# A graph network on one core: small weight loads issued behind the prologue's rounds, the bias add on VectorE tile by tile, and scatters behind the last gather without a wait for sums

## The chip, the cores and the metric

The kernel runs on one core of a Trainium2 chip. It is one program with five instruction streams: TensorE (PE, matrix products), VectorE (DVE), ScalarE (ACT), GpSimd (POOL) and SyncE (SP, which only issues transfers). Each stream runs in the order in which it is written, and the streams meet at semaphores. The metric is the device time of one execution in microseconds (us); lower is better.

## The reference

Four graph layers follow each other on 3750 nodes with 256 features and 63750 edges sorted by destination. Each layer normalises the nodes, clips at zero, computes something over the edges and adds it to `x`:

```
h = relu(layernorm(x));  x = x + L0(h, src, dst, edge_type)    # attention over 8 relations, 4 heads, + h_bias
h = relu(layernorm(x));  x = x + L1(h, ...)                    # graph convolution to 10 clusters, softmax
h = relu(layernorm(x));  x = x + L2(h, edge_attr, ...)         # edge net, sum over neighbours, 3-layer net
h = relu(layernorm(x));  x = x + L3(h, ...)                    # mean over neighbours, two products

feat_all = einsum('ni,rhid->rnhd', h, conv_weights)            # L0
e     = leaky_relu(el[type, src] + er[type, dst]);  alpha = softmax of e over the edges of one dst
out   = segment_sum(alpha * feat_all[type, src], dst) + h_bias
```

The change touches the beginning (L0's table and the dense adjacency matrix) and the scatters that fill this matrix.

## The kernel before, in words

Nodes stand in NT = 30 tiles of 128, edges in T = 500 tiles of 128. The work that matters here comes in this order.

**Load and normalise.** SP loads the edges, `x` and the attention weights. GpSimd writes zeros over the adjacency matrix `a_d` in DRAM (30 stores of 1088 KB, line 556; semaphore `a_zero`). ScalarE normalises the 30 node tiles (line 632), TensorE turns each (`turn_ring`, line 896; semaphore `n0_tp`) and computes the attention columns (line 928), VectorE copies the turned tiles (line 1453) and between them works on one-row masks (`follow_rows`, line 1403). GpSimd adds `h_bias` to all of `X` at once (line 561, 128x7680) as soon as ScalarE has read `X`, and stores the sum as `xb_d` (line 592; semaphore `x_out`).

**The prologue's rounds.** 50 rounds of 10 edge tiles. For a round SP loads two broadcast rows of `rel_d` (`rel_rows`) and one of `key_d` (`key_rows`); all SP loads have line 360. From the first VectorE makes one half of a one-hot matrix (`dst_one_hot`, line 1514) and ScalarE the other (lines 652 and 653). TensorE multiplies it (lines 965 and 966), and in the same stream computes the 120 parts of the feature table (line 954), which ScalarE copies out (line 667) and stores as `feat_d` (line 674). VectorE reduces (line 1533), counts equal edges (line 1520) and writes the values `VAL` (line 1527; semaphore `val_ready`). The loads for a round are issued when the one-hots two rounds before have been made. GpSimd scatters the values into `a_d`, four tiles a round, 200 in all (line 575); the first waits for `a_zero`, each fourth for `val_ready`. SP's twelve loads of small weights (`small_in`: W1A, EW2, CE, GB, COL, COL8) are issued ahead of the first `key_rows`, and VectorE waits for all twelve ahead of the first round. The four loads into COL8 have elements of 4 bytes, 1024 to a load.

**The gathers.** When all of `feat_d` is written and the 200 scatters are issued, GpSimd gathers the source rows of the 500 edge tiles (line 586) into a ring of 60 and, from tile 85 on, issues two scatters among five gathers. The other engines do softmax, messages and sums behind it, 20 tiles to a batch (DVE line 1671 adds the sums of a tile). Behind the last gather stand the 133 scatters left, each of which waits until one more tile has been summed (`agg_ps`).

**Behind that** the sums are turned home into `X`, the layer of clusters multiplies the adjacency matrix, which SP loads from `a_d` (line 360 into BG), and the edge network and the last layer follow.

The lines are those of the profile before.

Of the kernel before, what the change touches and what calls it, by code (L numbers as in the profile page):

```python
# [13 lines left out]
P = 128  # L14
# [3 lines left out]
ALU = mybir.AluOpType  # L18
ACT = mybir.ActivationFunctionType
# [27 lines left out]
def gnn(nc, x, src, dst, edge_attr, edge_type, conv_w, attn_l, attn_r, h_bias, gcn_w, gcn_b, cluster,  # L47
        eps, ee_w1, ee_b1, ee_w2, ee_b2, w1, b1, g1, be1, w2, b2, g2, be2, w3, b3, bn_g, bn_b,
        gamma, beta, w_l, b_l, w_r, out):
    N, D = x.shape  # L50
# [7 lines left out]
    NT = -(-N // P)  # L58
# [12 lines left out]
    NB = 20  # L71
# [17 lines left out]
    with ExitStack() as ctx:  # L89
# [184 lines left out]
        def s(name):  # L274
            if name not in S:
                S[name] = sem(name)
            return S[name]
# [71 lines left out]
        def bc(ap, shape):  # L349
            return ap.broadcast_to(shape)  # L350
# [7 lines left out]
        def _(sp):  # L358
# [53 lines left out]
                    rel_rows(u, u, h)  # L412
            for h in range(H):
                softmax_rows(h)
            with nc.allow_non_contiguous_dma(reason="small weight columns"):
                load(W1A[0:ED, :], ee_w1, "small_in")
                load(W1A[ED:ED + 1, :], ee_b1.rearrange("(o n) -> o n", o=1), "small_in")
                load(EW2[:, :, :], ee_w2.rearrange("(c p) n -> p c n", p=P), "small_in")
                load(CE[:, :], cluster, "small_in")
                load(GB[:, :], row(gcn_b, P), "small_in")  # L420
                load(B2C, ee_b2.rearrange("(c p) -> p c", p=P), "small_in")
                load(B1C, ee_b1.rearrange("(c p) -> p c", p=P), "small_in")
                load(SC2, eps.partition_broadcast(P), "small_in")
                for i, a in enumerate((g1, be1, g2, be2)):
                    load(COL8[:, i, :], a.rearrange("(c p) -> p c", p=P), "small_in")
# [5 lines left out]
            with sp.Fori(1, IT // 2) as w:  # L431
                for b in range(2):
# [5 lines left out]
                    sp.wait_ge(s("val_ready"), u + 1)  # L438
                    key_rows(u, b)

            sp.wait_ge(s("x_out"), 16)
            for v in range(NE):
                if v >= 3:
# [97 lines left out]
        def _(pool):  # L541
# [14 lines left out]
                pool.dma_start(rows(a_d, t).rearrange("p (a n) -> p a n", a=2),  # L556
                               bc(ZRO.unsqueeze(1), [P, 2, AD // 2])).then_inc(s("a_zero"), 16)

            pool.wait_ge(s("hb_in"), 16)
            pool.wait_ge(s("n0_hr"), NT)  # L560
            pool.tensor_tensor(X[:, :, :], X[:, :, :], bc(HB.unsqueeze(1), [P, NT, D]), ALU.add).then_inc(s("x_biased"), 1)
            pool.wait_ge(s("n0_tp"), NT)
            step(pool.memset(SEL, 0.0))
            for a in range(3):
# [8 lines left out]
            def scatter(t):  # L573

                pool.indirect_dma_start(  # L575
                    a_d.rearrange("n (w o) -> (n w) o", o=1), bass.IndirectOffsetOnAxis(ap=IDXS[:, t:t + 1], axis=0),
                    VAL[:, t:t + 1], None,
                ).then_inc(a_set[chunk_of(t)], 16)
                if t in CHUNKS[1:4]:
                    pool.wait_ge(a_set[chunk_of(t)], 16)  # L580
# [7 lines left out]
                    bass.IndirectOffsetOnAxis(ap=IDXST[:, t:t + 1], axis=0),  # L588
                ).then_inc(rows_in[t // NB % 3], 16)

            pool.wait_ge(s("x_biased"), 1)
            pool.dma_start(xb_d.rearrange("(t p) d -> p t d", p=P), X[:, :, :]).then_inc(s("x_out"), 16)
            pool.wait_ge(s("a_zero"), 16 * NT)
            for t in range(SOON):
                if t % CT == 0:
                    pool.wait_ge(s("val_ready"), t // CT + 3)
                scatter(t)
            pool.wait_ge(s("dve_mark"), DVE_MARKS["er_all"])
            pool.wait_ge(s("idx_ready"), 2)
# [9 lines left out]
            for t in range(T):  # L609
                gather(t)  # L610
                if t >= LEAD and (t - LEAD + 1) * 2 // 5 > (t - LEAD) * 2 // 5:
                    scatter_late(counted)
                    counted += 1
            for i, n in enumerate(range(counted, TR)):
                pool.wait_ge(s("agg_ps"), 20 + min(T - 3 * NB + 2 + i, T))
                scatter_late(n)
            pool.wait_ge(s("l3_d"), 7 * (NJ - 1) + 1)
            pool.memset(SG, 0.0).then_inc(s("acc_zero"), 1)  # L618
# [2 lines left out]
        def _(act):  # L621
# [52 lines left out]
                act.dma_start(rows(feat_d, t), STAGE[:, i, :, :].rearrange("p r n -> p (r n)")).then_inc(s(f"stage_out{i}"), 16)  # L674

            assert highs == 2 * IT
            act.wait_ge(s("small_in"), 16 * 12)
            act.activation(B1C, B1C, ACT.Relu).then_inc(s("b1_relu"), 1)
            for i in range(2):
                act.wait_ge(s(f"stage_out{i}"), 16 * NJ)  # L680
            act.wait_ge(s("cont_ready"), 1)
# [34 lines left out]
                edge_relu(0, q)  # L716
            soft_exp(0)
            soft_take(0)
            for b in range(NS):
                act.wait_ge(s("ex_sb"), b + 1)  # L720
                for k in range(NB):
                    v = (NB * b + k) // 4
                    if b + 1 < NS and k == 12:
                        soft_exp(b + 1)
                    for q in range(H):
                        m = RING[:, b % 3, k, q * DH:(q + 1) * DH]
                        last = act.activation(m, m, ACT.Copy, scale=EXT[:, b % 2, k, 1 + q:2 + q])  # L727
                    last.then_inc(s("msg_ready"), 1)
                    if k % 4 == 0 and v >= 1:
                        edge_relu(v, 1)  # L730
                    if k % 4 == 2 and v + 1 < NE:
                        edge_relu(v + 1, 0)
                    if k % 4 == 3 and v + 2 < NE:
                        edge_turned(v + 2)
                    if b + 1 < NS and k == 16:
                        soft_take(b + 1)
# [157 lines left out]
        def _(pe):  # L894
# [167 lines left out]
            pe.wait_ge(s("dve_mark"), DVE_MARKS["edge_start"])  # L1062
            net_turn(0)
            net_turn(1)
            for q in range(2):
                hidden(0, q)
            for part in (soft_turn, soft_ends, soft_carry, soft_back):
# [288 lines left out]
        def _(dve):  # L1356
# [189 lines left out]
                    counts(u + 1, following[0])  # L1546
                    values(u + 1)

            dve.wait_ge(s("small_in"), 16 * 12)
            for h in range(2):  # L1550
                dst_one_hot(0, h, 0, 0)
            counts(0, 0)
            values(0)
            for u in range(IT - 1):
                er_step(u, ((u + 1) % 2, (u + 1) // 2))
            er_step(IT - 1)

            dve.wait_ge(s("x_out"), 16)
# [175 lines left out]

            def home():

                step(ts(TILE0, IOTA[0:LT, 0:NT], -float(P), None, ALU.mult))
                attention_weights()
                dve.wait_ge(s("x_back0"), 16)
# [314 lines left out]
```

## Time and profile before

| | us |
|---|---|
| median of three runs | 3149.1 |
| lowest and highest | 3144.74 and 3156.03 |
| the profiled execution | 3144.03 |
| its span, first to last instruction | 3142.2 |

The granted TensorE clock was 0.937 of full speed on average. Busy shares of the span, from the page:

| engine | busy us | share |
|---|---|---|
| TensorE products | 2824.6 | 90% |
| VectorE | 1831.0 | 58% |
| ScalarE | 1405.3 | 45% |
| GpSimd | 1043.2 | 33% |

A busy share over the whole program says little here, since the stages have different limits: the page's 40 slices show 9 tenths for TensorE nearly everywhere, except in the first two slices (78.6 us each), which read 3 and 4. GpSimd reads 6 to 7 from the fourth slice to the seventeenth and almost nothing behind the nineteenth. The transfer engines read 8, 9, 7, 7 in the first four slices. The change works in the first six slices and between the seventeenth and the nineteenth. The small numbers in square brackets in a row are idle time of the engine just before the instruction, and the arrow names what ended it.

### The profile page before, as it was taken

How to read it: one execution, taken by the hardware profiler on the slowest of the kernel's cores; microseconds unless marked ns; L12 is line 12 of the kernel's file. 1: busy time of each engine (PE TensorE's matmuls, PEld its weight loads, DVE VectorE, ACT ScalarE, POOL GpSimd, SP SyncE). 2: the span in 40 equal slices, each digit the busy share in tenths (PEclk: the TensorE clock that was granted, in tenths of full speed). 3: DMA queues.
4: the chain of work that ended last, by engine and by line, in shares of the span. 5: the costliest groups of instructions: out<-in, count | busy, mean ns of one | idle time of the engine just before them, and what ended most of it. 6: DMA issues, size and time to landing. Idle time of an engine off the chain costs nothing.

```text
span 3142.2 us, 47689 instructions
## 1 busy us (share of the span) xinstructions
PE 2824.6 (90%) x14970; PEld 1862.6 (59%) x15034; DVE 1831.0 (58%) x5208; ACT 1405.3 (45%) x3883; POOL 1043.2 (33%) x1049
## 2 busy tenths in 40 slices
PE   3499958999999999988679998899999999999998
PEld 2344427899999888874144444555555555545446
DVE  7487866888888777775054333355555555513334
ACT  2077866778777888852032000244444444400000
POOL 4266677777777777777000000000000000000000
PEclk6599978999999999977869999999999999999999
DMA  8977754333333333216814333200000000132232
GB/s 295 343 219 204 223 158 117 96 94 95 93 94 92 93 93 94 68 54 181 253 63 123 101 103 98 75 5 7 3 7 5 5 7 3 49 101 68 84 101 79
DMA packets 245039, 317.67 MB, mean 101 GB/s; under 512 B 117627, under 2 KB 165924, under 8 KB 240740
## 3 DMA queue, kind: packets, MB, share of 16 engines
q1 hardware_dynamic: 191412, 179.07, 20.7%
q0 software_dynamic: 49104, 104.11, 11.1%
q10 hardware_dynamic: 4320, 31.95, 2.6%
q8 instruction: 108, 1.77, 0.2%
q14 instruction: 95, 0.78, 0.1%
HBM read 237.42 MB, written 77.59 MB: 100 GB/s over the span
## 4 chain that ended last, share of the span: by engine, by line
PE 63%; DVE 12%; ACT 7%; issue 5%; DMA 5%; SPq 4%; DVEq 3%; POOL 1%; POOLq 0%
PE PS L1237 17%; PE PS L1080 15%; PE PS L954 7%; PE PS L1046 5%; PE PS L1021 4%; PE PS L1059 4%; SPq L360 3%; PE PS L896 3%; DMA BG<-a_d 3%; ACT BG L727 3%; DVE BG L1805 2%; DVEq L1686 2%; DVE SUMS L1671 2%; ACT SL L810 1%; POOL BG L586 1%
## 5 line engine op out<-in xcount | busy, mean ns | idle before, releaser
L575 POOL DMA_INDIRECT a_d<-VAL,IDXS x499 | 501.1, 1004 | 236.9 <-issue 146.0
L1237 PE MATMUL PS<-BG,SL 128*128 128x512 f32 (+1 forms) x1440 | 538.4, 530 | 12.2 <-ACT SL L810 12.2
L586 POOL DMA_INDIRECT BG<-feat_d,IDXST x500 | 490.4, 981 | 155.7 <-issue 127.0
L727 ACT ACTIVATE BG<-BG,SL 128x64 f32<-128x64 f32 x2000 | 513.6, 337 | 0.0
L1671 DVE TENSOR_TENSOR SUMS<-SUMS,PS 128x640 f32 x500 | 409.0, 818 | 156.6 <-PE PS L1021 138.8
L1237 PEld LDWEIGHTS PS<-BG,SL 128*128 128x128 f32 x1440 | 276.4, 194 | 251.8 <-issue 222.4
L618 POOL MEMSET BG<- 128x7680 f32 x1 | 6.5, 6498 | 1254.5 <-DVE MV L1936 1254.5
L1021 PE MATMUL PS<-OHB,BG 128*128 128x128 f32 x2000 | 332.0, 289 | 0.0
L1059 PE MATMUL PS<-OHB,X 128*128 128x128 f32 x2000 | 312.2, 279 | 1.7 <-DVEq L1649 1.7
L1059 PEld LDWEIGHTS PS<-OHB,X 128*128 128x128 f32 x2000 | 282.6, 192 | 14.0 <-issue 1.7
L1046 PE MATMUL PS<-W1A,X 65*128 65x256 f32 x1000 | 271.2, 394 | 4.1 <-ACT X L701 0.9
L1021 PEld LDWEIGHTS PS<-OHB,BG 128*128 128x128 f32 x2000 | 264.5, 193 | 0.1
L797 ACT ACTIVATE SM<-SM,EPSC 128x1 f32<-128x1 f32 x60 | 17.7, 295 | 541.9 <-DVE SM L1897 541.9
L954 PE MATMUL PS<-SUMS,BG 128*128 128x512 f32 x480 | 240.1, 631 | 0.4 <-DVE CW L1498 0.4
L708 ACT ACTIVATE X<-PS 128x512 f32<-128x512 f32 x250 | 148.9, 595 | 118.1 <-PE PS L1046 116.7
L1080 PE MATMUL PS<-AL,BG 128*128 128x512 bf16 (+1 forms) x906 | 192.2, 368 | 5.4 <-DVE SUMS L1860 3.0
L1080 PE MATMUL PS<-AL,SUMS 128*128 128x512 bf16 (+1 forms) x893 | 188.2, 365 | 5.4 <-DVE X L2008 3.2
L1046 PEld LDWEIGHTS PS<-W1A,X 65*128 65x128 f32 x1000 | 172.1, 192 | 29.0 <-ACT X L701 9.4
L896 PE MATMUL PS<-IDENT,X 128*128 128x128 f32 (+3 forms) x650 | 145.1, 269 | 46.0 <-ACT X L701 15.4
L810 ACT ACTIVATE SL<-PS,COL 128x128 f32<-128x128 f32 x480 | 174.1, 476 | 25.5 <-PE PS L896 25.4
L1805 DVE TENSOR_TENSOR SUMS<-SUMS,OHB 128x2 f32 x499 | 81.7, 164 | 159.7 <-issue 93.4
L1805 DVE TENSOR_TENSOR BG<-BG,OHB 128x2 f32 x499 | 81.7, 164 | 144.7 <-issue 86.2
(305 smaller groups left out, 4172.7 us busy)
## 6 DMA issues: line engine op xcount, KB each, us to landing
BG<-a_d SPq DMA_DIRECT2D x141, 256.0 KB, 4.2
AL<-a_d SPq DMA_DIRECT2D x137, 256.0 KB, 2.6
a_d<-BG POOLq DMA_DIRECT2D x30, 1088.0 KB, 43.3
feat_d<-SUMS ACTq DMA_DIRECT2D x30, 1040.0 KB
BG<-rel_d SPq DMA_DIRECT2D x100, 160.0 KB
X<-in_edge_attr_dram SPq DMA_DIRECT2D x124, 128.0 KB
SUMS<-a_d SPq DMA_DIRECT2D x52, 256.0 KB, 2.6
SL<-key_d SPq DMA_DIRECT2D x50, 256.0 KB
```

What stands on the lines that cost most here:

```text
L575: pool.indirect_dma_start(a_d.rearrange("n (w o) -> (n w) o", o=1), bass.IndirectOffsetOnAxis(ap=IDXS[:, t:t + 1], axis=0), VAL[:, t:t + 1 ...
L586: pool.indirect_dma_start(RING[:, t // NB % 3, t % NB, :], None, feat_d.rearrange("n (r d) -> (n r) d", r=R), bass.IndirectOffsetOnAxis(ap ...
L727: last = act.activation(m, m, ACT.Copy, scale=EXT[:, b % 2, k, 1 + q:2 + q])
L896: return pe.transpose(out_ap, in_ap, IDENT[0:k, 0:k])
L954: last = pe.matmul(PS[:, 4 + q, :], HT[:, c, t * P:(t + 1) * P], WALL[:, c, q * 512:(q + 1) * 512], start=(c == 0), stop=(c == 1))
L1021: last = pe.matmul(at[:, (c + 1) * P:(c + 2) * P], RING[:, b % 3, k, c * P:(c + 1) * P], OH[:, k % 10, :], start=True, stop=True)
L1046: last = pe.matmul(EDGE_HIDDEN[:, k * D:(k + 1) * D], EAT[v % 2][:, 2 * q + k, :], W1A[:, :], start=True, stop=True)
L1059: pe.matmul(SUM_AT[n % 3][:, (3 + c) * P:(4 + c) * P], HM[v % 2][:, k, c * P:(c + 1) * P], OH[:, n % 10, :], start=True, stop=True)
L1080: last = pe.matmul(PS[:, 4 * (g % 2) + 2 * c + o // 512, 0:m], lhs(t, part)[:, c * P:(c + 1) * P], rhs[:, o:o + m], start=(t == 0 and part ...
L1237: last = pe.matmul(PS[:, to + q, 0:width], lhs[:, i, c, :], w[:, c, q * width:(q + 1) * width], start=(c == 0), stop=(c == kc - 1))
L1671: add = tt(a, a, SUM_AT[n % 3].rearrange("p (a n) -> p a n", a=5), ALU.add)
L1805: step(tt(a, a, held[:, :, n:n + 1], ALU.add))
```

## The change

1. SP issues the twelve small weight loads behind the rounds' loads, ahead of the wait for `x_out`. Who needs them waits for them later: TensorE ahead of the first product of the edge net, ScalarE ahead of the first messages (its clip of B1C moves there too), VectorE at the beginning of `home()`.
2. The bias add leaves GpSimd. VectorE adds it tile by tile, one add of 128x256 in each of the first 30 rounds, behind the values of the round. Ahead of the first round VectorE now waits for `hb_in` and for all of `n0_hr`.
3. The store of `xb_d` moves from ahead of the first scatter to ahead of scatter 128.
4. The 133 scatters behind the last gather lose their wait for `agg_ps`.

```
@@ SP
-            with nc.allow_non_contiguous_dma(reason="small weight columns"):
+            def small_weights():
                 load(W1A[0:ED, :], ee_w1, "small_in")
...
                     key_rows(u, b)
+            with nc.allow_non_contiguous_dma(reason="small weight columns"):
+                small_weights()
             sp.wait_ge(s("x_out"), 16)
@@ GpSimd
-            pool.wait_ge(s("hb_in"), 16)
-            pool.wait_ge(s("n0_hr"), NT)
-            pool.tensor_tensor(X[:, :, :], X[:, :, :], bc(HB.unsqueeze(1), [P, NT, D]), ALU.add).then_inc(s("x_biased"), 1)
...
-            pool.wait_ge(s("x_biased"), 1)
-            pool.dma_start(xb_d.rearrange("(t p) d -> p t d", p=P), X[:, :, :]).then_inc(s("x_out"), 16)
             pool.wait_ge(s("a_zero"), 16 * NT)
             for t in range(SOON):
                 if t % CT == 0:
                     pool.wait_ge(s("val_ready"), t // CT + 3)
+                if t == CT * (NT + 2):
+                    pool.wait_ge(s("x_biased"), NT)
+                    pool.dma_start(xb_d.rearrange("(t p) d -> p t d", p=P), X[:, :, :]).then_inc(s("x_out"), 16)
                 scatter(t)
...
-            for i, n in enumerate(range(counted, TR)):
-                pool.wait_ge(s("agg_ps"), 20 + min(T - 3 * NB + 2 + i, T))
+            for n in range(counted, TR):
                 scatter_late(n)
@@ ScalarE
-            act.wait_ge(s("small_in"), 16 * 12)
-            act.activation(B1C, B1C, ACT.Relu).then_inc(s("b1_relu"), 1)
...
             soft_take(0)
+            act.wait_ge(s("small_in"), 16 * 12)
+            act.activation(B1C, B1C, ACT.Relu).then_inc(s("b1_relu"), 1)
@@ TensorE
             net_turn(1)
+            pe.wait_ge(s("small_in"), 16 * 12)
@@ VectorE
-            dve.wait_ge(s("small_in"), 16 * 12)
+            dve.wait_ge(s("hb_in"), 16)
+            dve.wait_ge(s("n0_hr"), NT)
...
             for u in range(IT - 1):
                 er_step(u, ((u + 1) % 2, (u + 1) // 2))
+                if u < NT:
+                    tt(X[:, u, :], X[:, u, :], HB, ALU.add).then_inc(s("x_biased"), 1)
...
             def home():
+                dve.wait_ge(s("small_in"), 16 * 12)
```

SP's stream before, from behind the twelve loads of `dst` to the first loads of the rounds (SL<-key_d is `key_rows`, BG<-rel_d is `rel_rows`):

```order
L360 DMA W1A<-in_L_gnn_ee_w_dram 64x256
L360 DMA W1A<-in_L_gnn_ee_b_dram 1x256
L360 DMA EW<-in_L_gnn_ee_w_dram 128x2x256
L360 DMA CE<-in_L_gnn_cluster_emb_dram 10x256
L360 DMA GB<-in_L_gnn_bias_dram 128x10
L360 DMA COL<-in_L_gnn_ee_b_dram 128x2x1 x2
L360 DMA COL<-in_L_gnn_eps_dram 128x1
L360 DMA COL<-in_L_gnn_g_dram 128x8x1
L360 DMA COL<-in_L_gnn_be_dram 128x8x1
L360 DMA COL<-in_L_gnn_g_dram 128x8x1
L360 DMA COL<-in_L_gnn_be_dram 128x8x1
L360 DMA SL<-key_d 128x512 [waits key_out,n0_tp]
```

The same place in the changed stream:

```order
L360 DMA SUMS<-in_dst_dram 18x128
L360 DMA SUMS<-in_dst_dram 1x6
L360 DMA SL<-key_d 128x512 [waits key_out,n0_tp]
L360 DMA SL<-key_d 128x512
L433 UNCONDITIONAL_BRANCH
L433 ISA
L360 ISA [waits oht_high,oht_ready]
L360 DMA BG<-rel_d 128x640
```

The twelve loads are gone from between the `dst` loads and the first key rows; they stand behind the branch that ends the loop.

GpSimd before, from the zero stores to the first scatters (a_d<-VAL,IDXS):

```order
L556 DMA a_d<-BG 256x1x2176 x29
L561 TENSOR_TENSOR X<-X,BG 128x7680 [waits n0_hr,hb_in]
L563 MEMSET SL 80x384 [waits n0_tp]
L565 AFFINE_SELECT SL<-SL 80x128 [waits pool_steps] x3
L569 AFFINE_SELECT SL<-SL 80x128 [waits pool_steps] x2
L571 MEMSET SL 128x200 [waits pool_steps]
L592 DMA xb_d<-X 128x30x256 [waits x_biased]
L575 DMA a_d<-VAL,IDXS 16711680x1 [waits val_ready,a_zero]
```

GpSimd in the changed kernel at the same place:

```order
L560 DMA a_d<-BG 256x1x2176 x29
L564 MEMSET SL 80x384 [waits n0_tp]
L566 AFFINE_SELECT SL<-SL 80x128 [waits pool_steps] x3
L570 AFFINE_SELECT SL<-SL 80x128 [waits pool_steps] x2
L572 MEMSET SL 128x200 [waits pool_steps]
L576 DMA a_d<-VAL,IDXS 16711680x1 [waits val_ready,a_zero]
```

The large add and the store of `xb_d` are gone from between the zeros and the scatters. 

VectorE in the changed kernel, the end of one round and the beginning of the next (L1529 writes the values, L1560 is the bias add, L1535 the reduction of the next round):

```order
L1542 TENSOR_TENSOR OHB<-OHB,SUMS 128x320 [waits oht_ready]
L1545 TENSOR_REDUCE AL<-OHB 128x40 [waits dve_steps]
L1522 TENSOR_SCALAR SL,BG<-SL,BG 128x128 [waits dve_steps]
L1522 TENSOR_SCALAR SL,BG<-SL,BG 128x128 x3
L1529 CAST VAL<-BG 128x4 [waits dve_steps]
L1560 TENSOR_TENSOR X<-X,BG 128x256
L1535 TENSOR_REDUCE OHB<-PS 128x160 [waits er_ps]
```

The row L1560 is new; the others stand as before, two lines lower.

## Rows read from the trace of the kernel before

**Rows 1.** Chain of waits, 40 to 150 us: start, duration, what.
```profile
112.72 32.79 DMA COL<-in_L_gnn_be_dram
```
**Rows 2.** Timeline of VectorE ahead of the rounds: start, duration, engine, line, idle before.
```profile
74.55 13.49 DVE L1403 TENSOR_TENSOR BG<-OHB,BG 1x500 f32<-1x500 f32 x1
...
111.53 0.66 DVE L1504 CAST BG<-BG 128x960 bf16<-128x960 f32 x1
145.53 0.39 DVE L1514 TENSOR_SCALAR SUMS<-BG,IOTP 128x640 bf16<-128x640 bf16 x1 [33.34 <-DMA COL<-in_L_gnn_be_dram]
```
**Rows 3.** Timeline of TensorE and ScalarE, same stretch.
```profile
90.01 0.66 PE L896 MATMUL PS<-IDENT,SL 128*128 128x128 f32 x2 [6.13 <-DVE BG L1453]
...
146.37 0.83 ACT L652 ACTIVATE SUMS<-BG,IOTP 128x640 bf16<-128x640 bf16 x1 [74.12 <-DMA SL<-key_d]
```
**Rows 4.** Timeline of GpSimd and of SP's queue.
```profile
70.91 16.60 POOL L561 TENSOR_TENSOR X<-X,BG 128x7680 f32<-128x7680 f32 x1 [7.54 <-ACT SL L632]
96.81 0.41 POOL L563 MEMSET SL<- 80x384 f32 x1 [9.30 <-PE PS L896]
99.70 1.66 POOL L592 DMA_DIRECT2D xb_d<-X  x1
149.06 1.06 POOL L575 DMA_INDIRECT a_d<-VAL,IDXS  x1 [47.70 <-DVE VAL L1527]
...
77.69 0.58 SPq L360 DMA_DIRECT2D W1A<-in_L_gnn_ee_w_dram  x1
...
421.56 0.33 SPq L360 DMA_DIRECT2D SL<-key_d  x1
```
**Rows 5.** Transfer queues, 45 to 60 us: packets, MB, share of 16 engines.
```profile
q0 software_dynamic: 1252, 5.14, 84.6%
q1 hardware_dynamic: 981, 0.86, 17.1%
```
**Rows 6.** The same, 100 to 134 us, and the landing of the last two zero stores.
```profile
q0 software_dynamic: 3335, 13.63, 98.2%
q1 hardware_dynamic: 3335, 0.01, 5.5%
...
a_d<-BG POOLq DMA_DIRECT2D x2, 1088.0 KB, 75.0
```
**Rows 7.** The same queues during the rounds, 147 to 438 us.
```profile
q1 hardware_dynamic: 22320, 28.71, 43.3%
q10 hardware_dynamic: 4176, 30.89, 26.7%
q0 software_dynamic: 6290, 0.06, 1.6%
```
**Rows 8.** The 200 scatters of line 575, 147 to 442 us: their durations and waits.
```profile
L575 POOL DMA_INDIRECT a_d<-VAL,IDXS x200: 962/967/1272, 149.1 to 440.2; - x100
...
  DVE VAL L1527: 85.1, 26
```
**Rows 9.** From the rounds to the first sum: chain of waits and timelines.
```profile
437.69 3.92 DMA feat_d<-SUMS
...
442.43 0.99 POOL L586 DMA_INDIRECT BG<-feat_d,IDXST  x1 [1.28 <-DMA feat_d<-SUMS]
...
466.64 0.36 ACT L700 ACTIVATE X<-PS 64x256 f32<-64x256 f32 x1
...
485.93 0.82 DVE L1671 TENSOR_TENSOR SUMS<-SUMS,PS 128x640 f32 x1 [0.21 <-PE PS L1021]
```
**Rows 10.** VectorE adds of two SBUF operands: ns min/median/max, first and last start.
```profile
L1540 DVE TENSOR_TENSOR OHB<-OHB,SUMS x49: 491/493/540, 155.3 to 433.5; 128x320 f32<-128x320 f32 x49
...
L1733 DVE TENSOR_TENSOR X<-X,SL x30: 391/416/475, 1399.8 to 1438.4; 128x256 f32<-128x256 f32 x30
```
**Rows 11.** GpSimd's waits behind the last gather, 1306.5 to 1487 us: us, times, longest.
```profile
POOL a_d L575 <- PE PS L1021: 3.7, 12, 0.3
```
**Rows 12.** TensorE waiting for the adjacency matrix.
```profile
1505.95 2.74 PE L1172 MATMUL PS<-BG 128*30 128x512 bf16 x6 [16.35 <-DMA BG<-a_d]
```

## The prediction

> **What bounds the kernel now.** I read three views in this order. The page's slices say that TensorE is busy nearly everywhere except in the first two slices, so a loss is to be sought there. The chain of waits then names it: one piece of 32.79 us is the landing of a load into COL8 [rows 1]. The timelines of the engines in the stretch from 60 to 150 us show what stood still. VectorE ended its preparation at 111.53 + 0.66 = 112.2 us and began the first round at 145.53, and the load named is one of the twelve small ones [rows 2]. ScalarE began its share of the second half round only at 146.37, ended by the first key row, which stood behind the small loads in the same queue [rows 3]. So 33.3 us pass with no engine at work, and both causes, the wait for weights that no round uses and the place of the key rows, are taken away by the same part of the change.
>
> The queue rows say why the loads are slow. From 100 to 134 us the zero stores hold the engines at 98.2%, and queue 1 moves as many packets as queue 0, 3335 against 3335, though its own are of a few bytes: 0.01 MB [rows 6]. One packet of the one goes with one of the other. The small loads are some 5,200 packets by the shapes in the code, four times 1024 of them COL8; at 3335 packets in 34 us, 98 a us, that is 53 us.
>
> Behind the rounds the gathers are the next bound: the first starts when `feat_d` has landed, and the first sum comes 485.93 - 442.43 = 43.5 us later [rows 9]. From there on GpSimd and TensorE keep each other's pace, and I take all that follows as shifted whole.
>
> **Start of the rounds.** GpSimd's large add runs from 70.91 for 16.60 us [rows 4]. In it stands a one-row VectorE operation that took 13.49 us [rows 2], and behind this one TensorE waited 6.13 us for a turned tile [rows 3]. Without the add the TensorE stream, which is the longer, moves up by these 6.1 us, and with it the end of VectorE's preparation: 112.2 - 6.1 = 106.1. The new waits of the first one-hot (`hb_in`, all of `n0_hr`) are long over: the last row read ended before the add began at 70.91. The key rows are issued when the last node tile is turned, 96.81 - 6.1 = 90.7 [rows 4]; they are 256 packets, some 4 us at the pace above even with the zeros beside them, and what is left of the `dst` loads ahead of them. They land before 106. If they didn't, each us would be a us of the end. The rounds start 145.5 - 106.1 = 39.4 us earlier.
>
> **What is late next: the zeros.** Scatters must wait for the zeros. Their last stores took 75 us to land, from about 63, so 138 [rows 6]; the first scatter, at 149.06, waited for VectorE's values [rows 4]. Now the rounds begin 32 us ahead of that landing and their loads and table stores compete with the zeros. Zero work left at 106 is 0.98 x (138 - 106 - 3), about 28 us of all 16 engines. Bounds: if the zeros lost nothing they would land at 138 as before. If they got only what the rounds' queues leave when alone, 100 - 43.3 - 26.7 = 30% [rows 7], they would need 28 / 0.30 = 93 us and land at 199. Between them I work out one round per engine, one packet against one. Queue 1 moves 22320 / 50 / 16 = 28 packets a round [rows 7], each with a zero packet beside it of 98.2% x 34 x 16 / 3335 = 0.160 us [rows 6]: 4.5 us. Its own packets take 0.042 us when the engines are full, 17.1% x 15 x 16 / 981 [rows 5]: 1.2 us. Queue 10 has 4176 / 50 / 16 = 5.2 packets of 26.7% x 291 x 16 / 4176 = 0.30 us [rows 7]: 1.5 us. Sum 7.2 us, of which the zeros have 62%: 28 / 0.62 = 45 us, landing at 151. This value I take, since it lies nearest to [rows 5], where queue 0 kept 84.6% beside a busy queue 1 and no queue 10.
>
> **GpSimd's scatters.** From 149.1 to 441.2 they took 292.1 us, 85.1 of which were waits for values, 47.7 of these ahead of the first [rows 4, 8]. So 37.4 us of waits lie within, in which 25 issue gaps of 0.3 would stand anyway: own pace 292.1 - 29.9 = 262 us. Now the rounds run six rounds ahead at the start and take 5.84 us against 5.2 for four scatters, so GpSimd hardly ever waits. End: 151 + 262 + 1.7 for the store of `xb_d` [rows 4] = 415. The store itself, 3840 KB, takes the queues some 10 us around the 34th round; it lies beside rounds that are loaded two ahead.
>
> **End of the rounds.** They took 437.7 - 145.5 = 292 us. At 7.2 instead of 5.84 us for the 45 us of overlap, less the two rounds loaded before, they lose 6 us. The bias adds are 30 of 0.416 us, 12.5 us of VectorE by the same shape [rows 10]. They stand behind the values, ahead of a reduction for which VectorE often waits; bounds 0 and 12.5, I take 2. End 106 + 292 + 8 = 406, and 3.9 more until `feat_d` has landed [rows 9]: 410. So GpSimd, not the table, sets the first gather: 415 instead of 442.4, **27 us earlier**. Before, the order was the other way round.
>
> **Small loads in the new place.** SP issues them behind the last key row, before at 421.56 [rows 4], now some 32 us earlier, 390. At the slow pace they would take until 443, and the edge loads behind them; ScalarE wants the first at 466.64 - 27 = 440 [rows 9]. But queue 0 then moves only scatters, 1.6% [rows 7], so they land well before. Cost nothing; with that cover gone, up to 5 us. The clip of B1C, its wait and the wait in `home()` stand where they were long met.
>
> **Scatters behind the last gather.** GpSimd's waits for TensorE there are 12 of at most 0.3 us [rows 11], which is the gap between any two scatters. The sums were always far enough ahead, so the removed wait was never the later one. Gain 0.
>
> **Sum.** 3144.0 - 27 = 3117 against the profiled execution. That one stands 5.1 us below the median of the three runs, so the forecast is 3149.1 - 27 = 3122.
>
> **Rivals.**
> *Full gain.* The zeros lose nothing and the rounds aren't slowed: GpSimd ends at 138 + 262 + 2 = 402, the table has landed at 106 + 292 + 4 = 402, gain 40, 3109. For it: the engines serve packets of few bytes for nothing today. Against it: the rounds' packets are of 1 to 8 KB.
> *The adds block on GpSimd.* The add that goes was in the way of VectorE. If the new adds, of two SBUF operands, had to wait each for a scatter in flight (0.967 us, [rows 8]), they would cost 30 x 0.97 = 29 us on VectorE; the rounds would end at 404 + 29 = 433, first gather 437, gain 5, 3144. Against it: line 1540 has two SBUF operands too and ran beside the scatters at 491 to 540 ns, 49 times [rows 10]. The Trainium skill, SBUF — State Buffer (the list of practical consequences behind the doors), has the rule that a VectorE instruction with two SBUF inputs contends with a GpSimd instruction that reads SBUF and that the later one blocks fully. By that rule the trace agrees for the large add, and for scatters it depends on whether issuing one reads SBUF in that sense; the rows say no.
> *The zeros starve (slower).* If the rounds' queues were served first, the zeros would land at 199, the scatters end at 199 + 262 + 2 = 463, and the first gather would come 21 us later than now: 3170. It decides from a landing behind 178. Against it: equal packet counts [rows 6]. The Trainium skill, DMA: Bandwidth & Descriptors (Queues, rings and completion order), says that each engine goes round the queues that have work; by that the zeros can't starve, and the counts agree.
> *The stall in reading the adjacency matrix goes.* TensorE waited 16.35 us for one load there [rows 12], close to the end of the scatters. If it hangs on how scatters and loads fall together it may go: 3122 - 16 = 3106. Against it: both move together.
>
> **Chances.** Forecast 0.71, own range 3111 to 3137 (landing of the zeros between 140 and 162, the adds 0 to 12, the runs' own scatter of some 5 us). Full gain 0.14, adds block 0.05, zeros starve 0.03, stall gone 0.07. A change of 0.3%, 9.4 us, is about what a measurement of this kernel can tell from none. Faster by more: 0.70 of the forecast's 0.71, full gain and stall gone, 0.91; within it: 0.05; slower: 0.04, the starving and a little for what I don't see. The range that holds the time 8 times in 10 is 3104 to 3138.
>
> **What would show it.** The first one-hot at 106 us without a named wait of more than 1 us ahead; the one-row operation of line 1403 at 0.66 us both times; the first scatter at 151, ended by a landing of the zeros and no longer by values; its rounds at 7 us until then and 5.8 after; first gather at 415, with GpSimd's own instruction right ahead of it; first sum at 458; GpSimd's spacing behind the last gather unchanged at 1.27. The prediction is wrong if the first scatter comes behind 165 or the first gather doesn't follow the last scatter, and if the stretch from the first gather to the end isn't 2700 us as before.

## The result, and the profile after

The changed kernel takes 3118.2 us (median; 3110.6 to 3123.1), the kernel before 3149.1 us beside it. The ratio is 0.9896, 95% interval 0.9873 to 0.9919: faster by 1.0%, 31 us by the medians. Forecast were 3122 us and 27 us. The profiled execution took 3116.4 us with a span of 3114.6, so the spans of the two profiles differ by 27.6 us.

The total came out near the forecast, but two of the steps behind it did not. I go through the profile after in the order of [rows 2] to [rows 12]. Its lines have moved by one to five numbers (L1403 is now L1405, the first one-hot L1516, the scatters L576, the gathers L587, the sums L1676).

Timeline of VectorE ahead of the rounds, which answers to [rows 2]:

```profile
70.39 0.66 DVE L1405 TENSOR_TENSOR BG<-OHB,BG 1x500 f32<-1x500 f32 x1
74.37 0.66 DVE L1405 TENSOR_TENSOR BG<-OHB,BG 1x500 f32<-1x500 f32 x1
106.03 0.81 DVE L1516 TENSOR_SCALAR SUMS<-BG,IOTP 128x640 bf16<-128x640 bf16 x2 [0.38 <-DVE BG L1506]
```

The one-row operation takes 0.66 us both times, where one of the two took 13.49, and the first one-hot comes at 106.0 us (forecast 106.1) with no wait for a load ahead of it. The start of the rounds is won in full: 39.5 us.

Timeline of SP's queue and of GpSimd, and the group of the 200 early scatters with its waits [rows 4, 8]:

```profile
90.24 1.59 SPq L360 DMA_DIRECT2D SL<-key_d  x2
...
146.00 1.27 POOL L576 DMA_INDIRECT a_d<-VAL,IDXS  x1 [52.81 <-DMA a_d<-BG]
```

```profile
L576 POOL DMA_INDIRECT a_d<-VAL,IDXS x200: 952/958/1275, 146.0 to 415.8; - x100
...
  DVE VAL L1529: 15.0, 19
```

The first scatter now waits for the zeros, as forecast, but they land at 146, not at 151. It is followed by 15.0 us of waits for VectorE's values, where I had expected hardly any: GpSimd catches up with the rounds, which are the slower partner.

Chain of waits, 410 to 420 us (start, duration, what), then the last early scatter, the first gather and the first sum by the timelines [rows 9]:

```profile
413.00 0.60 ACT SUMS L668
413.60 0.02 issue
413.62 3.92 DMA feat_d<-SUMS
417.54 0.02 issue
417.56 0.04 POOLq L603
417.61 0.77 issue
418.38 0.99 POOL BG L587
```

```profile
415.81 0.96 POOL L576 DMA_INDIRECT a_d<-VAL,IDXS  x1 [0.30 <-issue]
418.38 0.99 POOL L587 DMA_INDIRECT BG<-feat_d,IDXST  x1 [1.60 <-DMA feat_d<-SUMS]
...
461.92 0.82 DVE L1676 TENSOR_TENSOR SUMS<-SUMS,PS 128x640 f32 x1 [0.27 <-PE PS L1022]
```

The first gather is at 418.4, not at 415, and what it waits for is the landing of the table. GpSimd's last scatter ended at 416.8, 1.6 us too soon to matter. So the table still sets this point, as before, and the gain here is 442.43 - 418.38 = 24.0 us, not 27. The other 3.6 us of the span's 27.6 come later.

Where did 39.5 become 24? The start of one VectorE operation in every round (line 1540 before, 1542 now; its 50 starts) shows it. These are some of its starts in both kernels, which I took from the timelines, with the gap to the round before (us):

| round | before | after | gap before | gap after |
|---|---|---|---|---|
| 0 | 155.25 | 114.79 | | |
| 1 | 160.04 | 125.55 | 4.8 | 10.8 |
| 2 | 164.81 | 130.67 | 4.8 | 5.1 |
| 3 | 170.24 | 140.77 | 5.4 | 10.1 |
| 34 | 350.43 | 318.89 | 5.5 | 4.8 |
| 35 | 357.30 | 333.49 | 6.9 | 14.6 |
| 49 | 438.25 | 414.18 | 4.8 | 5.1 |

The lead is 40.5 us at round 0, 29.5 at round 3, 31.5 at round 34, 23.8 at round 35 and 24.1 at the last. Between round 3 and round 34 nothing is lost, 2 us are even regained: two places cost 11.0 and 7.7 us. Windows of the changed kernel (from and to, length, then the busy us of PE, PEld, DVE, ACT and POOL, then the granted clock, the share of the DMA engines and GB/s), and the same 15 us of the kernel before:

```profile
106.00:141.00 35.00, 29.18 (x120) 14.53 (x121) 19.09 (x64) 17.55 (x27) 0.00 (x0) 0.80 1.02 414
146.00:313.00 167.00, 160.72 (x852) 81.51 (x853) 141.24 (x460) 128.39 (x202) 124.41 (x128) 0.98 0.75 216
319.00:334.00 15.00, 8.97 (x40) 4.57 (x39) 5.16 (x16) 5.03 (x10) 11.34 (x13) 0.77 0.97 355
```

```profile
319.00:334.00 15.00, 15.00 (x87) 7.95 (x87) 12.04 (x43) 12.08 (x21) 9.14 (x10) 1.00 0.75 208
```

In both places the DMA engines are full, in the first from the zeros, in the second from the store of `xb_d`, which GpSimd issues at 313.96:

```profile
313.96 1.67 POOL L598 DMA_DIRECT2D xb_d<-X  x1
...
325.15 0.26 PE L966 MATMUL PS<-BG,SUMS 128*128 x1 [6.03 <-issue]
326.70 0.66 DVE L1535 TENSOR_REDUCE OHB<-PS 128x160 f32<-128x480 f32 x1 [5.17 <-PE PS L967]
```

```profile
xb_d<-X POOLq DMA_DIRECT2D x1, 3840.0 KB, 19.9
```

The store landed in 19.9 us, not in 10. TensorE stood 6.0 us in one piece; the granted clock was 0.77 over the window.

Queues of the changed kernel, 100 to 134 us, beside [rows 6]:

```profile
q0 software_dynamic: 2765, 11.32, 80.9%
q1 hardware_dynamic: 1274, 1.74, 13.9%
q10 hardware_dynamic: 144, 1.07, 7.4%
```

These windows begin 6 us ahead of the rounds. The model's 62% is a mean from the start of the rounds to the landing, and so is this view, 106 to 146 us:

```profile
q0 software_dynamic: 2590, 10.58, 64.3%
q1 hardware_dynamic: 2126, 2.90, 20.1%
q10 hardware_dynamic: 288, 2.13, 12.8%
```

The zeros had 64.3% of the engines on the mean, close to the model, and their share fell from 86.5% (106 to 120 us) to 66.3% (120 to 134) and 36.2% (134 to 146). What was smaller than forecast is the work that was left at 106: 64.3% of 40 us is 25.7 us of all engines, not 28.

The small loads are issued at 399.6 to 409.0, not from 390, since the rounds end later than forecast. No engine's wait names them; ScalarE's first reader ran at 457.7, behind a wait for TensorE. TensorE's wait for the adjacency matrix [rows 12] is there still, in two pieces, and GpSimd behind the last gather shows no wait for TensorE at all [rows 11]:

```profile
1473.29 1.03 PE L1174 MATMUL PS<-BG 128*30 128x512 bf16 x2 [10.35 <-DMA BG<-a_d]
1481.35 1.89 PE L1174 MATMUL PS<-BG 128*30 128x512 bf16 x4 [5.03 <-DMA BG<-a_d]
```

```profile
POOL a_d L576 <- issue: 42.7, 140, 0.3
```

### The profile page after: what moved, and what is told of

Read it like the earlier page. It is cut to its first block, busy times and chain, and to the rows that moved or that the text cites. A ratio compares the mean times of both kernels' runs of the same rounds, so it can differ in the third digit from the quotient of the medians.

```text
span 3114.6 us, 47712 instructions
## 1 busy us (share of the span) xinstructions
PE 2823.0 (91%) x14970; PEld 1865.5 (60%) x15034; DVE 1827.9 (59%) x5238; ACT 1404.4 (45%) x3883; POOL 1021.0 (33%) x1048
## 4 chain that ended last, share of the span: by engine, by line
PE 59%; DVE 19%; ACT 7%; issue 6%; DMA 4%; DVEq 3%; POOL 1%; SPq 0%; POOLq 0%
PE PS L1239 17%; PE PS L1082 15%; PE PS L955 6%; DVE SUMS L1676 4%; DMA BG<-a_d 4%; PE PS L1047 3%; ACT BG L728 3%; PE PS L897 3%; PE PS L1022 3%; PE PS L1060 3%; DVE BG L1811 2%; DVEq L1691 2%; DVE X L1682 2%; ACT SL L811 1%; DVE OHB L1628 1%
## 5 line engine op out<-in xcount | busy, mean ns | idle before, releaser
L576 POOL DMA_INDIRECT a_d<-VAL,IDXS x499 | 492.3, 987 | 220.5 <-issue 149.5
L587 POOL DMA_INDIRECT BG<-feat_d,IDXST x500 | 493.6, 987 | 157.8 <-issue 126.1
L1676 DVE TENSOR_TENSOR SUMS<-SUMS,PS 128x640 f32 x500 | 409.0, 818 | 156.1 <-PE PS L1022 140.1
L897 PE MATMUL PS<-IDENT,X 128*128 128x128 f32 (+3 forms) x650 | 145.0, 268 | 45.8 <-ACT X L700 15.4
```

The costliest lines, as they stand in the source:

```text
L576: pool.indirect_dma_start(a_d.rearrange("n (w o) -> (n w) o", o=1), bass.IndirectOffsetOnAxis(ap=IDXS[:, t:t + 1], axis=0), VAL[:, t:t + 1 ...
L587: pool.indirect_dma_start(RING[:, t // NB % 3, t % NB, :], None, feat_d.rearrange("n (r d) -> (n r) d", r=R), bass.IndirectOffsetOnAxis(ap ...
L897: return pe.transpose(out_ap, in_ap, IDENT[0:k, 0:k])
L1676: add = tt(a, a, SUM_AT[n % 3].rearrange("p (a n) -> p a n", a=5), ALU.add)
```

## The experiments

The theory after the result: the load order frees the start, the bias edit a further 7 us of it; 11 us go back to the zeros in rounds 1 and 3 and 7.5 to the late store in round 35; the bias adds and the waits behind the last gather cost nothing; what differs behind the first sum is the clock.

**e1_load_order.** The kernel before with part 1 alone. Against the changed kernel it lacks the bias edit and part 4, and the store of `xb_d` stands in its old place ahead of the first scatter (the lines of the store and of part 4 are left out here):

```diff
+            pool.tensor_tensor(X[:, :, :], X[:, :, :], bc(HB...), ALU.add).then_inc(s("x_biased"), 1)
...
-                if u < NT:
-                    tt(X[:, u, :], X[:, u, :], HB, ALU.add).then_inc(s("x_biased"), 1)
```

> The kernel before with the load order alone changed: small loads behind the key rows, the waits for them where their first readers stand. GpSimd's large bias add, the early store of xb_d and the sum waits behind the last gather stay as before. Theory (the load order frees the 33 us, contention gives part back): the rounds start at 112 us, since the add still holds the preparation up by 6 us; the first scatter comes at about 145 with the zeros; the store of xb_d follows the zeros in queue 0 and takes the engines some 10 us more among early rounds. Rounds end at 112 + 292 + about 14 = 418, first gather at 423, 19 us sooner than before: 3130 us. Rival (the repaired bias is what pays, half of the gain or more): under 13 us, over 3136. Rival (the late store of xb_d costs the changed kernel 7 us that the early one does not): 27 us sooner, 3122 or less, as fast as the changed kernel.

Measured: 3134.2 us, ratio to the kernel before 0.9958 (0.9943 to 0.9973). VectorE's timeline, the first scatter and the first gather:

```profile
75.19 13.48 DVE L1407 TENSOR_TENSOR BG<-OHB,BG 1x500 f32<-1x500 f32 x1
...
113.10 0.81 DVE L1518 TENSOR_SCALAR SUMS<-BG,IOTP 128x640 bf16<-128x640 bf16 x2 [0.28 <-DVE BG L1508]
```

```profile
136.73 1.05 POOL L578 DMA_INDIRECT a_d<-VAL,IDXS  x1 [34.73 <-DMA a_d<-BG]
...
426.87 0.99 POOL L589 DMA_INDIRECT BG<-feat_d,IDXST  x1 [1.58 <-DMA feat_d<-SUMS]
```

With the large add back, the 13.48 us are back and the rounds start 7.1 us later. The store behind the zeros is not free either: rounds 1 and 3 took 12.9 and 14.5 us here, in the changed kernel 10.8 and 10.1, which is 6.5 us more and near the 7.7 that the late store costs. Here the zeros landed at 136.7, and round 3 ended its 14.5 us at 155.2, behind that landing and beside the store, whose queue had 58.2% of the engines from 137 to 145 us. That the early store is the cause is argued from this order, not shown apart. At the first gather (15.6 us sooner than before, of 24.0) the bias edit is worth 8.5 us. I had expected 19 us there and 3130 us; the early rounds lost more than I gave them. Neither rival holds. By the times e1 is 16 us behind the changed kernel, more than the 8.5; see what stays open.

**e2_no_sum_waits.** The kernel before with part 4 alone:

```diff
-            for i, n in enumerate(range(counted, TR)):
-                pool.wait_ge(s("agg_ps"), 20 + min(T - 3 * NB + 2 + i, T))
+            for n in range(counted, TR):
```

> The kernel before with only the waits of the late scatters for the sums of TensorE taken away. Theory (these waits were always met): no difference, 3149 within 3 us, last scatter at 1484 as before. Rival (the waits held the scatters up now and then, or the scatters run ahead and crowd the reads): the last scatter moves by 4 us or more, and the time with it, to either side.

Measured: 3147.7 us, ratio 0.9993 (0.9980 to 1.0006). The last scatters of it, and of the kernel before:

```profile
1485.66 0.97 POOL L575 DMA_INDIRECT a_d<-VAL,IDXS  x1 [0.30 <-issue]
1486.93 0.97 POOL L575 DMA_INDIRECT a_d<-VAL,IDXS  x1 [0.30 <-issue]
```

```profile
1483.24 0.97 POOL L575 DMA_INDIRECT a_d<-VAL,IDXS  x1 [0.30 <-issue]
1484.51 0.97 POOL L575 DMA_INDIRECT a_d<-VAL,IDXS  x1 [0.30 <-issue]
```

The gaps of 0.30 us and the spacing of 1.27 are the same, and the last scatter is 2.4 us later rather than earlier. These waits cost nothing that the runs can tell.

**e3_adds_out.** The changed kernel without the 30 adds (the output lacks that bias):

```diff
-                    tt(X[:, u, :], X[:, u, :], HB, ALU.add).then_inc(s("x_biased"), 1)
+                    dve.engine_nop().then_inc(s("x_biased"), 1)
```

> The changed kernel with the 30 bias adds of VectorE left out (the output lacks that bias; the counts of the semaphore stay). Theory (the adds lie in VectorE's idle time within a round): the rounds end within 1 us of 413.6, time 3118 within 3 us. Forecast's term: 2 us faster. Rival (VectorE paces the rounds): up to 12 us faster, 3106.

Measured: 3119.4 us, ratio 0.9906 (0.9887 to 0.9926). The first gather, and the adds of the changed kernel, which are absent here:

```profile
418.96 0.98 POOL L587 DMA_INDIRECT BG<-feat_d,IDXST  x1 [1.46 <-DMA feat_d<-SUMS]
```

```profile
L1560 DVE TENSOR_TENSOR X<-X,BG x30: 415/418/420, 117.3 to 294.9; 128x256 f32<-128x256 f32 x30
```

418.96 without and 418.38 with them: the 12.5 us of adds on VectorE delay nothing. The shortest rounds are 5.1 us with the adds and 4.8 without, but round 7 is 6.3 with them and 8.3 without, and by round 34 both stand at 318.9 us. The durations of the adds, 415 to 420 ns, leave no room for a wait of a whole scatter (0.96 us).

**e4_store_split.** The changed kernel with the store in six pieces from SP (the waits for `x_out`, now for six stores, are left out here):

```diff
-                if t == CT * (NT + 2):
-                    pool.wait_ge(s("x_biased"), NT)
-                    pool.dma_start(xb_d.rearrange("(t p) d -> p t d", p=P), X[:, :, :]).then_inc(s("x_out"), 16)
...
+            for upto, t0, t1 in [(3, 0, 5), (6, 5, 10), (8, 10, 15), (11, 15, 20), (13, 20, 25), (16, 25, 30)]:
+                loaded(at, upto + 1)      # the rounds' loads up to this pair of rounds
+                at = upto + 1
+                sp.wait_ge(s("x_biased"), t1)
+                sp.dma_start(xb_d[t0 * P:t1 * P, :]..., X[:, t0:t1, :]).then_inc(s("x_out"), 16)
```

> The changed kernel with the store of xb_d, 3840 KB in one piece by GpSimd ahead of scatter 128, cut into six stores of 640 KB that SP issues behind rounds 7, 13, 17, 23, 27 and 33. Theory (the one store fills the DMA engines for 20 us, the rows of a round come late, and round 35 loses 7.4 us): no round over 9 us any more behind the zeros, the last round's copy at 406 instead of 413, first gather at 411, time 3111. Rival (the rounds lose as much in six small pieces, since the same bytes are moved): no gain, 3118. Rival (GpSimd ends at 415.8 + 1 whatever the table does): gain of 2 us, 3116.

Measured: 3115.5 us, ratio 0.9894 (0.9875 to 0.9914). The landing of four of the six, the first gather and the first sum:

```profile
xb_d<-X SPq DMA_DIRECT2D x4, 640.0 KB, 6.6
```

```profile
412.77 0.99 POOL L596 DMA_INDIRECT BG<-feat_d,IDXST  x1 [2.04 <-DMA feat_d<-SUMS]
...
456.22 0.82 DVE L1682 TENSOR_TENSOR SUMS<-SUMS,PS 128x640 f32 x1 [0.27 <-PE PS L1028]
```

Round 35 takes 7.1 us instead of 14.6, and the first gather and the first sum come 5.6 and 5.7 us sooner: the late store is what round 35 lost by. GpSimd's last scatter moved too, its end from 416.8 to 410.7, so the rival that GpSimd ends where it did whatever the table does fell. Yet the time of 3111 that I expected did not come, and the span, 3115.1, is not shorter. 4.4 us of it went in one place, which the windows of this kernel show, with the matching work of the changed kernel under it:

```profile
671.00:678.00 7.00, 7.00 (x29) 6.56 (x30) 1.28 (x5) 2.80 (x12) 5.33 (x6) 0.50 0.37 95
```

```profile
679.00:686.00 7.00, 7.00 (x57) 6.73 (x56) 5.12 (x14) 5.34 (x21) 5.17 (x7) 1.00 0.31 82
```

The granted clock is at its lower level, 1.2 GHz, for 7 us, and 29 matmuls are done against 57. Ahead of it TensorE had run at the upper level, with a gap of 1.36 us at 666.2; the changed kernel has a gap of 1.49 us at the same work without a fall.

**e5_zeros_paced.** The split store, and the last seven zero stores paced by the rounds:

```diff
+            for k in range(7):
+                pool.wait_ge(s("val_ready"), 3 + k)
+                zero_rows(NT - 7 + k)
             pool.wait_ge(s("a_zero"), 16 * NT)
```

> The kernel with the split store (e4_store_split), and of the 30 zero stores of GpSimd the last seven are issued one by one behind the values of rounds 0 to 6, where all 30 stood in the queue from 46 us on. Same bytes. Theory (rounds 1 and 3 lose 11 us because the zeros hold the engines until 146, and a zero store a round of 2.7 us fits beside a round's own transfers): the standing 23 stores end near 119, round 3 no longer takes 10 us, the zeros land at 146 to 152, the rounds end 5 us sooner than in e4_store_split and the first gather comes at 408 instead of 412.8, where GpSimd's scatters begin to bind: 3111. Rival (each paced store delays its round as much as before): no gain, 3115. Rival (the landing of the zeros moves back and GpSimd sets the end): slower, 3120 and first scatter behind 155.

Measured: 3132.3 us, ratio 0.9955 (0.9939 to 0.9970), slower than e4_store_split. My theory fell and its last rival came true, more strongly than priced. GpSimd's timeline, the last of the seven paced stores first:

```profile
154.78 0.68 POOL L570 DMA_DIRECT2D a_d<-BG  x1 [5.21 <-DVE VAL L1542]
166.15 1.04 POOL L589 DMA_INDIRECT a_d<-VAL,IDXS  x1 [10.70 <-DMA a_d<-BG]
...
432.19 0.96 POOL L589 DMA_INDIRECT a_d<-VAL,IDXS  x1 [0.30 <-issue]
433.46 1.13 POOL L600 DMA_INDIRECT BG<-feat_d,IDXST  x1 [0.30 <-issue]
```

Round 1 took 8.5 us, 2.6 less than in e4_store_split, but round 3 still took 12, the last stores went out late, and round 7 took 14.6 beside the last of them and the first piece of the split store, which landed in 15.9 us. The zeros landed 20 us later than in the changed kernel, and now GpSimd's own instruction stands right ahead of the first gather. This run also measures GpSimd's own pace: 166.2 to 433.2 is 267 us with 1.5 us of waits for values (forecast 262). So pacing the zeros by the rounds put round 7 7.2 us behind e4_store_split's and the first scatter 20 us later. Whether another order would bring zeros at 146 for less than the 11 us of rounds 1 and 3 is not shown.

**e6_small_first.** The changed kernel with the small loads ahead of the key rows again, the late waits kept:

```diff
+                small_weights()
             sp.wait_ge(s("n0_tp"), NT)
             sp.wait_ge(s("key_out"), 16)
```

> The changed kernel with the twelve small loads issued where they stood before, ahead of the key rows; the waits for them stay with their late readers. It parts the two causes of the 33 us. Theory (the place of the key rows in the queue holds the rounds as long as the wait did): the first one-hot of half round 0 comes at 106, that of half 1 at 144 to 146, ended by a landing of key_d; the late store still costs its 7 us; so no gain is left, 3149 to 3153. Rival (the wait of VectorE was the cause and the order of the loads is of no account): 3118.

Measured: 3136.1 us, ratio 0.9959 (0.9944 to 0.9975). ScalarE's second half round, GpSimd's first scatter and first gather:

```profile
135.77 0.83 ACT L653 ACTIVATE SUMS<-BG,IOTP 128x640 bf16<-128x640 bf16 x1 [62.35 <-DMA SL<-key_d]
```

```profile
138.47 1.05 POOL L576 DMA_INDIRECT a_d<-VAL,IDXS  x1 [43.93 <-DVE VAL L1529]
...
434.22 0.98 POOL L587 DMA_INDIRECT BG<-feat_d,IDXST  x1 [1.34 <-DMA feat_d<-SUMS]
```

The place of the key rows alone holds the rounds up to 135.8, with VectorE's wait already gone, and the first gather comes 15.8 us later than in the changed kernel: the order of the loads counts. Without it, the rest of the change brings 8.2 of the 24.0 us at the first gather. I had said 144 to 146, and 3149 to 3153 us, since I carried over the landing of [rows 2]; but there the store of `xb_d` kept the engines full behind the zeros, and here it does not. Rounds 1 to 3, all behind the zeros, took 6.1, 5.3 and 5.3 us, and round 35 again 14.6. This is the control for both losses: without zeros beside the rounds there is no loss in rounds 1 and 3, and with the late store round 35 loses as before. The profiled execution, 3122.8 us, is the fastest of the seven here, 13 us below the median, so the profile explains the first gather and not the median.

**e7_changed_again** and **e8_before_again.** Both kernels unaltered.

> The changed kernel, unaltered, for a second profile. Theory (the 3.6 us by which the stretch behind the first sum is shorter in its first profile are short falls of the granted clock that come and go): from the first weighted message of the edge network to the end between 1472 and 1481 us, first sum again at 462 within 1 us. Rival (the change shortens that stretch by itself): again 1472 within 1 us, 4 us less than the kernel before.

> The kernel before, unaltered, for a second profile. Theory: first sum at 486 within 1 us, the stretch of the edge network to the end between 1472 and 1481 us, where the first profile has 1476.1. Rival: 1476 within 1 us again, and the difference to the changed kernel is of the change.

Measured: e7 3114.4 us, ratio 0.9892 (0.9876 to 0.9908), with a profiled span of 3121.5; e8 3146.4 us. The first gathers are at 421.2 and 440.6, the first sums at 464.6 (2.6 away, not within 1) and at 484.1 (1.8 away). The stretch that begins with the first matmul of line 1082 (1080 before) and ends with the first of L1353 took 1475.7 and 1479.9 us, in the first profiles 1471.9 and 1476.1. So the rival, 1472 and 1476 again within 1 us, fell: the stretch varies by nearly 4 us between profiles of one kernel. But both pairs differ by 4.2 us the same way, and the third profile of the changed kernel, below, has 1470.2, under the range I had named. That the 3.6 us are not the change's is not shown.

**e9_split_again** and **e10_changed_third.** The two side by side.

> The kernel with the split store once more, beside the changed kernel on the same chip. Theory (the 5.6 us won by the split in round 35 last; in its first profile one fall of the clock at 671 us took 4.4 us back): first sum at 457 within 1.5 us, no fall of the clock between 550 and 1340 us, 5 us faster than the changed kernel beside it. Rival (what the table wins is given back behind the first gather each time): the fall or another loss is there again, and the two are equal within 2 us.

> The changed kernel, unaltered, for the comparison with e9_split_again and a third profile: first sum at 462 to 465, round 35 again 14 to 15 us long, time 3114 to 3119.

Measured: 3119.8 us, ratio 0.9893 (0.9874 to 0.9911), and 3121.6 us, ratio 0.9908 (0.9886 to 0.9929); the intervals overlap. First gathers:

```profile
411.95 0.99 POOL L596 DMA_INDIRECT BG<-feat_d,IDXST  x1 [1.73 <-DMA feat_d<-SUMS]
```

```profile
418.72 0.98 POOL L587 DMA_INDIRECT BG<-feat_d,IDXST  x1 [1.63 <-DMA feat_d<-SUMS]
```

Round 35 of e10 took 14.4 us again. The split wins 6.8 us at the first gather, but 2 in the time instead of the 5 expected. The fall of the clock is there in both (0.74 from 660 to 675 us in e9, 0.69 from 675 to 690 in e10), in the changed kernel for the first time, so it is not the split's own. The theory for e9 fell and its rival came true: the fall is there again, and the two are equal within 2 us. The first sums came at 455.4 in e9 and 462.2 in e10, and e10's 3121.6 us lies above the 3114 to 3119 that I had named. So no version is shown to beat the changed kernel: the split is faster by 2.7 (against 3118.2) and 1.8 us in the median, which these runs can't tell from nothing; against the remaining median of the changed kernel, 3114.4 in e7, it isn't faster at all.

## Why the prediction was right, and where it was not

**Start of the rounds: right.** 106.0 for 106.1, the key rows issued at 90.2 for 90.7. e6 shows that the order of the loads was needed, e1 that the large add holds VectorE and so the start: 7.1 us of it for the 6.1 forecast.

**The zeros: mechanism right, size off.** 146 for 151. The share of 62% measured 64.3%; the work left at 106, priced at 28 us, measured 25.7, and 25.7 / 0.62 would give a landing at 147.5. The round of packets is thus a fair model for the mean over the stretch, though the share fell on the way. The 138 for a landing with nothing lost was late as well: in e6, with no round beside the zeros, their queue fell from 83.3% of the engines (128 to 130 us) to 0.6% (134 to 136).

**End of the rounds: the term that was mis-sized.** Forecast were 292 + 8 us; the table's last copy ended at 413.6, 307.6 us behind the first one-hot. The 6 us for the contention with the zeros measured 11.0, beside a granted clock of 0.80. The store of `xb_d` was put at nothing, as lying "beside rounds that are loaded two ahead": it cost 7.7 us. The 2 us for the adds measured 0 (e3). The rest of the rounds gave some 3 us back, 2.1 of them between round 3 and round 34. So the rounds lost 15.4, not 8.

**What sets the first gather: the step that failed.** "So GpSimd, not the table, sets the first gather" is wrong; the table does, at 418.4. That the sum held is luck: two errors nearly made up for each other. With the zeros at 146 GpSimd's term falls from 415 to 410, and with the measured rounds the table's term rises from 410 to 418; the later of the two moved by 3 us only. The prediction had named a first gather that doesn't follow the last scatter as a sign of being wrong, and by this sign its mechanism at this point is wrong.

**Small loads and part 4: right**, 0 each, the second shown by e2.

**All behind shifted whole: right but for what the clock takes.** From the first gather to the end the kernel before took 2699.8 and 2704.0 us, the changed one 2696.2, 2700.4 and 2699.8. First sums stand at 461.9, 464.6 and 462.2 us in three profiles of the changed kernel and 485.9 and 484.1 in two of the one before: 22 us. Behind it the stretches differ by the granted clock. I summed width times (1 - clock) over windows of 50 us in the stretch of e7 and e8, an estimate of what the lower clock took:

| kernel | stretch, us | lost by the clock | rest |
|---|---|---|---|
| before | 1476.1 | 21.3 | 1454.8 |
| before again | 1479.9 | 23.4 | 1456.5 |
| e2_no_sum_waits | 1481.0 | 23.9 | 1457.1 |
| changed | 1471.9 | 16.9 | 1455.0 |
| changed again | 1475.7 | 21.8 | 1453.9 |
| changed, third | 1470.2 | 16.2 | 1454.0 |
| e1_load_order | 1480.8 | 26.9 | 1453.9 |
| e6_small_first | 1469.1 | 14.0 | 1455.1 |

The stretch varies by 11.9 us, the rest by 3.2; the other four profiles lie at rests of 1452.1 to 1453.9. So most of what differs in the stretch is clock. But each of the three profiles of the changed kernel is shorter there than each of the three that start as before, and no run shows whether that is the change's doing or chance.

**The rivals.** Full gain fell: the start came in full, but the zeros and the store took 18.7 us back. The blocked adds fell: 415 to 420 ns each. The starving zeros fell: they land at 146. The stall for the adjacency matrix did not go: it is 10.35 + 5.03 us, where it was 16.35.

**What stays open.** By the medians the changed kernel gained 31, 32 and 32 us in three comparisons, while three profiles against two (3118.2 and 3143.4 us on the mean) give 25, and the first sum 22. The mean granted clock of the runs is higher in the changed kernel (0.942, 0.942 and 0.940 in the three comparisons, against 0.935), but part of that is idle time that is gone (the clock stood at 0.54 in the idle 33.3 us of the kernel before), and no run here parts the two. The clock also bears on e1, which is 8.5 us behind the changed kernel at the first gather and 16 behind in the median. Its profile is 16.1 us longer (spans 3130.7 and 3114.6), and besides the 8.5 us it lost 8.9 in the stretch of the table, where the clock took 10.0 us more. Why the clock was lower there is not settled.

## What to carry to other kernels

When a start moves forward, ask what it now runs beside: here 39.5 us became 24 since the rounds met the zeros, and a store of 3840 KB moved among them cost 7.7 us while 30 vector adds cost none. A large transfer that nobody waits for still has a price where each step loads its own data. Cutting it in pieces took that price away here at the first gather, though the gain in the whole time was too small to be told from nothing. And where two partners end within 3 us of each other, a forecast of the time can hold although it names the wrong one: look at the instruction that stands right ahead of the point where they meet, and at what the next one waited for.

## What the runs showed of the hardware

One store of 3840 KB from GpSimd held the engines at a share of 0.97 for 15 us and cost one round 7.7 us; the same bytes in six stores from SP landed in 6.6 us by the median, and no round behind the zeros took over 8.6. One such piece, issued beside the last zero stores in e5, took 15.9 us. The packets of two busy queues were not always one for one: while the small loads ran beside the zeros in e6, 95 to 134 us, queue 1 moved 4731 packets and queue 0 3601, where [rows 6] have 3335 each. From 100 to 130 us alone, while the zeros still filled the engines, it was 3331 against 2938. The whole window:

```profile
q0 software_dynamic: 3601, 14.73, 91.8%
q1 hardware_dynamic: 4731, 0.20, 9.7%
```

A one-row operation of VectorE took 13.49 and 13.48 us beside a large GpSimd add and 0.66 without it. The Trainium skill, SBUF — State Buffer (the list of practical consequences behind the doors), has this contention, of a VectorE instruction with two SBUF inputs against a GpSimd instruction that reads SBUF. These runs agree for the add; beside GpSimd's scatters 30 adds of the same kind took 415 to 420 ns and show no such wait.
